# Where the output bias of an attention layer is added: in a TensorE bank, or in place by GpSimd

## The chip, the cores and the metric

The kernel runs on one core of one Trainium2 chip, in Bass: each engine's instructions are written out by hand in their order, and semaphores join them. The metric is the time of one launch in microseconds (us), as the median of several runs.

## The reference

A transformer block on x of 4096 rows (4 sequences of 1024) with 128 features, all in float32:

```
h  = layernorm(x)
q, k, v = h @ Wq + bq, h @ Wk + bk, h @ Wv + bv        # 16 heads of 8
q, k = q / |q|, k / |k|                                 # per head
attn = (q @ k.T) / 1024 ** sigmoid(m)                   # no softmax
x1 = x + (attn @ v) @ Wo + bo
h2 = layernorm(x1)
logits = h2 @ router.T                                  # 16 experts, one chosen per row
out = x1 + expert(h2 * sigmoid(top logit)) + shared(h2) # two gated MLPs
```

As there is no softmax, `(q @ k.T) @ v` is computed as `q @ (k.T @ v)`, with one masked 128x128 matrix per sequence that already holds Wo. The term of this case is `bo`, a row of 128 numbers that is added to every row of `x`.

## The kernel before, in words

The rows stand in 32 tiles of 128 rows, and four tiles make a quad; `c` is always a quad, 0 to 7. Two quads are one sequence. `xres` (128 partitions, 32 tiles, 128 features) holds x, later x1, and at last the output. Every step of a quad is a small function on one engine, and each engine calls these functions in an order written out by hand, the steps of several quads interleaved:

- VectorE: `x_stats(c)` (line 725) takes mean and variance of the quad's rows of `xres` with `bn_stats` and `bn_aggr` (lines 719 and 722) and raises `var1`. `take(c, h)` (line 757) scales half a quad's q, k and v out of PSUM and adds their biases. `head_sums` (765), `inv_norms` (770), `x1_stats` (735), `h_scales` (743) and, per quad, `choose` and `place`, which rank the rows for the experts, follow. `weights_lo(n)` (line 783) is done twice: it takes the low part of a weight matrix of the shared MLP, 128x512, from two tiles in SBUF. Of them, `weights_lo(0)` stands behind `x_stats(7)`, `h_scales(1)` and `mask_vk(1)`, and before `head_sums(4)`; `weights_lo(1)` behind `take(7, 1)`.
- GpSimd: some constants, then `scale_v` and `scale_q` (line 317), which multiply a quad's v and q by the inverse norms; `hT_lo` (327), `count` (334), `scatter` (343, one indirect DMA for a tile), and from 122 us `send` (352), 48 indirect DMAs.
- ScalarE: copies out of PSUM, square roots, `x1_copy(c)` (465), which brings x1 back from PSUM into `xres`, `norm_h(c)` (471), and the SiLU of the experts.
- TensorE: `project`, `v_by_k`, `fold_wo`, `turn_q`, `attend`, `turn_h`, `route`, then the matmuls of the MLPs. `free(after)` is a wait that makes sure that a PSUM bank may be written.

`attend(c)` builds x1 for a quad in one bank: a product of a column of ones with the row of biases (line 1148), a product of the identity with `xres` (1149), and q by the matrix (1154). For the first product VectorE prepares the bias once, in `bias_rows` (lines 892 to 900): as the product is made in float32r, the bias is split into a rounded row and the remainder, on two partitions. `bias_rows` stands behind `x_stats(0)` and `scale_mask()` follows it, then `x_stats(1)`.

The bias is loaded by ScalarE's DMA queue behind `m_col`, `w_qkv` and `w_o`. The queue of SP loads x and its transpose quad by quad. A wait on a semaphore holds all that its engine has behind it.

Of the kernel before, what the change touches and what calls it, by code (L numbers as in the profile page):

```python
# [7 lines left out]
ALU = mybir.AluOpType  # L8
ACT = mybir.ActivationFunctionType
AX = mybir.AxisListType  # L10
F32 = mybir.dt.float32
F32R = mybir.dt.float32r
I32 = mybir.dt.int32

P = 128


def build_block(nc, S, x, x_t, w_in, b_in, Wo, bo, m_col_in, router_t, gate_up, down, shared_gate, shared_up,
# [4 lines left out]
    _, NT, D = x.shape  # L23
# [6 lines left out]
    Q = 4  # L30
# [22 lines left out]
    with ExitStack() as ctx:  # L53
        def sb(name, shape, dt=F32):
            return ctx.enter_context(nc.sbuf_tensor(name, shape, dt))

        def sem(name):
            return ctx.enter_context(nc.semaphore(name))

        xres = sb("xres", [P, NT, D])  # L60
# [12 lines left out]
        ident = sb("ident", [P, P])  # L73
        before = sb("before", [P, P])
        ones = sb("ones", [P, P])
# [40 lines left out]
        with ExitStack() as attention:  # L116
            def sb_a(name, shape, dt=F32):
                return attention.enter_context(nc.sbuf_tensor(name, shape, dt))

            qkv = sb_a("qkv", [P, QRING, Q, QKV])  # L120
            sq = sb_a("sq", [P, Q, 2 * D])
            xT = sb_a("xT", [P, T])
            qT = sb_a("qT", [P, RING, Q * P])
            ss = sb_a("ss", [P, 2, Q, 2 * HEADS])
            rn = sb_a("rn", [P, 2, Q, 2 * HEADS])
            vkm = sb_a("vkm", [P, 2, D])
            wb = sb_a("wb", [P, 2, D])
            w_qkv = sb_a("w_qkv", [P, D + QKV])
            b_qkv = sb_a("b_qkv", [P, QKV])
            w_c = sb_a("w_c", [P, QKV])  # L130
            m_col = sb_a("m_col", [P, 1])
            m_tmp = sb_a("m_tmp", [P, 4])
            head_mask = sb_a("head_mask", [P, D])
            zeros = sb_a("zeros", [P, E, W])
            w_sh = sb_a("w_sh", [P, 2, SF])
            bo_in = sb_a("bo_in", [2, D])
            bo_top = sb_a("bo_top", [2, D], F32R)
            bo_two = sb_a("bo_two", [2, Q, D], F32R)
            two_col = sb_a("two_col", [2, 1])
            ones_r = sb_a("ones_r", [2, P], F32R)  # L140
        xg = sb("xg", [P, SLOTS, W])
        logit = sb("logit", [P, SLOTS])
        logit_silu = sb("logit_silu", [P, SLOTS])
# [11 lines left out]
        ps_hT, ps_qy, ps_vk, ps_log = bank  # L155
# [6 lines left out]
        ld_b, ld_bo, ld_wo, ld_wa = sem("ld_b"), sem("ld_bo"), sem("ld_wo"), sem("ld_wa")  # L162
        ld_rw, ld_sg, ld_su, ld_sd = sem("ld_rw"), sem("ld_sg"), sem("ld_su"), sem("ld_sd")

        k_col, k_id, k_pool, k_ids = sem("k_col"), sem("k_id"), sem("k_pool"), sem("k_ids")
# [2 lines left out]
        ach = sem("ach")  # L168
        m_step, mask_rdy = sem("m_step"), sem("mask_rdy")
        var1, std1, rstd1 = sem("var1"), sem("std1"), sem("rstd1")  # L170
        wc_mm, wc_rdy, bo_rdy = sem("wc_mm"), sem("wc_rdy"), sem("bo_rdy")
        hT_mm, hT_sb = sem("hT_mm"), sem("hT_sb")
        qkv_mm, qkv_sb, sq_done = sem("qkv_mm"), sem("qkv_sb"), sem("sq_done")
        ssum, floored, nrm, rn_rdy = sem("ssum"), sem("floored"), sem("nrm"), sem("rn_rdy")
# [93 lines left out]
        def _(pool):  # L268
            g = nc.gpsimd
# [5 lines left out]
            g.memset(before[:], 1.0)  # L275
            g.memset(ones[:], 1.0)
            g.memset(head_mask[:], 1.0)
            g.memset(two_col[:], 1.0)
            g.memset(run_mask[:], 1.0)
            g.memset(seen[:, 0], 0.0).then_inc(k_pool, 1)  # L280
            pool.wait_ge(k_pool, 1)
# [1 line left out]
                            pattern=[[-1, P]], channel_multiplier=1).then_inc(k_id, 1)  # L283

            g.affine_select(out=head_mask[:], in_=head_mask[:], compare_op=ALU.is_ge, fill=0.0, base=0,
                            pattern=[[-HD, HEADS], [0, HD]], channel_multiplier=1).then_inc(k_pool, 1)

            g.affine_select(out=before[:], in_=before[:], compare_op=ALU.is_gt, fill=0.0, base=0,
                            pattern=[[1, P]], channel_multiplier=-1)

            g.affine_select(out=two_col[:], in_=two_col[:], compare_op=ALU.is_gt, fill=0.0, base=0,
                            pattern=[[0, 1]], channel_multiplier=1)
            g.affine_select(out=run_mask[:], in_=run_mask[:], compare_op=ALU.not_equal, fill=0.0, base=0,
                            pattern=[[0, E], [1, Q]], channel_multiplier=0)
            pool.wait_ge(k_pool, 2)
# [2 lines left out]
                            pattern=[[HD, HEADS], [0, HD]], channel_multiplier=-1).then_inc(k_pool, 1)  # L298
# [20 lines left out]
            def scale_v(c):  # L319
                scale_heads(c, 2 * D, HEADS, v_rdy)  # L320

            def scale_q(c):
                scale_heads(c, 0, 0, q_rdy)

            def hT_lo(c):
                pool.wait_ge(hT_hi_rdy, c + 1)
                g.tensor_tensor(hT[:, 1, 512 * c:512 * c + 512], hT_full[:, 512 * c:512 * c + 512],  # L327
                                hT[:, 0, 512 * c:512 * c + 512].bitcast(F32), ALU.subtract).then_inc(hT_rdy, 1)
# [17 lines left out]
            def send(g):  # L346
                pool.wait_ge(yg_rdy, g + 1)
                for j in range(Q):
                    n = g * Q + j
                    if n >= 3:  # L350
# [2 lines left out]
                        out=y_back, out_offset=bass.IndirectOffsetOnAxis(ap=xg[:, n, D + 1:D + 2].bitcast(I32), axis=0),  # L353
                        in_=yg[:, g % YRING, j], in_offset=None, bounds_check=T - 1, oob_is_err=False).then_inc(y_sent[n % 3], 16)

            scale_v(0)
            scale_q(0)
            scale_v(1)
            scale_q(1)
            scale_v(2)  # L360
            scale_q(2)
            scale_v(3)
            scale_q(3)
            hT_lo(0)
            count(0)
            scale_v(4)
# [67 lines left out]
        def _(act):  # L434
# [1 line left out]
            act.dma_start(m_col[:], m_col_in).then_inc(ld_m, 16)  # L436
            act.dma_start(w_qkv[:], w_in).then_inc(ld_wa, 16)
            act.dma_start(w_o[:], Wo).then_inc(ld_wo, 16)
            act.dma_start(bo_in[:], bo.partition_broadcast(2)).then_inc(ld_bo, 16)
            act.dma_start(rwT[:], router_t).then_inc(ld_rw, 16)  # L440

            act.wait_ge(ld_m, 16)
# [265 lines left out]
        def _(dve):  # L708
            v = nc.vector
            links = [0]  # L710

            def link(ins):
                links[0] += 1
                ins.then_inc(dch, 1)
                dve.wait_ge(dch, links[0])
# [173 lines left out]
                dve.wait_ge(k_pool, 3)  # L889
                v.tensor_scalar(head_mask[:], head_mask[:], m_tmp[:, 3:4], None, ALU.mult).then_inc(mask_rdy, 1)  # L890

            def bias_rows():
                dve.wait_ge(ld_bo, 16)
                dve.wait_ge(k_ids, 1)
                v.tensor_copy(ones_r[:], ones[0:2, :])
                link(v.tensor_copy(bo_top[:], bo_in[:]))
                link(v.tensor_scalar(bo_top[:].bitcast(F32), bo_top[:].bitcast(F32), two_col[:], None, ALU.mult))
                v.tensor_tensor(bo_two[:], bo_in[:].unsqueeze(1).broadcast_to([2, Q, D]),
                                bo_top[:].bitcast(F32).unsqueeze(1).broadcast_to([2, Q, D]), ALU.subtract
                                ).then_inc(bo_rdy, 1)  # L900

            v.memset(zeros[:], 0.0).then_inc(z_done, 1)
            dve.wait_ge(ach, 1)
            link(v.tensor_scalar(m_tmp[:, 1:2], m_tmp[:, 0:1], 1.0, None, ALU.add))
            v.reciprocal(m_tmp[:, 2:3], m_tmp[:, 1:2]).then_inc(m_step, 1)
            x_stats(0)
            bias_rows()
            scale_mask()
            x_stats(1)
            x_scales(0)  # L910
# [183 lines left out]
        def _(pe):  # L1094
            te = nc.tensor
# [46 lines left out]
                last.then_inc(qT_mm, 1)  # L1142

            def attend(c, after=None):
                if c == 0:
                    pe.wait_ge(bo_rdy, 1)
                free(after)
                te.matmul(ps_qy[:], ones_r[:], bo_two[:].rearrange("p j d -> p (j d)"), start=True, stop=False)
                te.matmul(ps_qy[:], ident[:], xres[:, Q * c:Q * c + Q, :].rearrange("p j d -> p (j d)"), start=False,
                          stop=False)  # L1150
                pe.wait_ge(qT_sb, c + 1)
                pe.wait_ge(wb_rdy, c // QB + 1)
                for j in range(Q):
                    last = te.matmul(ps_qy[:, P * j:P * j + P], qT[:, c % RING, P * j:P * j + P], wb[:, c // QB % 2],
                                     start=False, stop=(j == Q - 1))
                last.then_inc(y_mm, 1)
# [334 lines left out]
```

## Time and profile before

| | |
|---|---|
| time, median of 3 runs | 216.1 us (215.64 to 216.8) |
| span of the profiled execution, first to last instruction | 212.6 us |
| the profiled execution's own time | not recorded beside its span; the median of the runs lies 3.5 us above the span |
| TensorE busy | 192.1 us (90%), 1126 matmuls |
| VectorE busy | 146.2 us (69%), 501 instructions |
| ScalarE busy | 103.2 us (49%), 234 instructions |
| GpSimd busy | 112.1 us (53%), 140 instructions |
| granted TensorE clock, mean | 0.998 of full speed |

The profile follows one execution. Busy time is the time in which an engine carried out an instruction; an engine's row of the timeline gives the start, the duration (of several instructions of one kind together, with their count), the line, the operation and the tiles, and in brackets how long the engine was idle before and what released it. PE is TensorE, DVE VectorE, ACT ScalarE, POOL GpSimd; a q behind an engine's name is its instruction queue.

### The profile page before, as it was taken

The numbers are of one execution on the slowest core, as the hardware profiler recorded it, in microseconds if no ns is written. First come the engines' busy times: TensorE is split into PE (matmuls) and PEld (weight loads), VectorE is DVE, ScalarE is ACT, GpSimd is POOL, SyncE is SP. The second block draws the span as 40 slices with busy tenths as digits, with TensorE's granted clock in tenths as the row PEclk, the third lists the DMA queues.
The fourth block names the chain that finished last, engine by engine and source line by source line (L and its number), as shares of the span: only waits on it lengthen the run. The fifth ranks groups of instructions, "written<-read, shape, count | busy, mean of one in ns | idle before, by whom it ended". The sixth has DMA issues, their size and how long they took to land.

```text
span 212.6 us, 3825 instructions
## 1 busy us (share of the span) xinstructions
PE 192.1 (90%) x1126; PEld 155.6 (73%) x1126; DVE 146.2 (69%) x501; ACT 103.2 (49%) x234; POOL 112.1 (53%) x140
## 2 busy tenths in 40 slices
PE   0896699999989899999988989999999999999992
PEld 0352556656767677888677979899999898889882
DVE  3679999999999977866535767946645333247553
ACT  3423464983567499773414556556653223122320
POOL 6002504357598787667720077777767777760000
PEclk9999999999999999999999999999999999999999
DMA  5999993000100101111125446621111110039243
GB/s 166 309 390 259 177 378 153 5 0 25 39 28 27 38 25 41 52 38 50 52 63 112 106 118 149 158 59 43 47 33 38 45 47 0 0 91 327 81 161 135
DMA packets 17607, 21.59 MB, mean 102 GB/s; under 512 B 3224, under 2 KB 11679, under 8 KB 17332
## 3 DMA queue, kind: packets, MB, share of 16 engines
q1 hardware_dynamic: 13872, 15.73, 26.4%
q0 software_dynamic: 2560, 4.24, 6.3%
q10 hardware_dynamic: 1156, 1.39, 1.9%
q8 instruction: 9, 0.15, 0.3%
q14 instruction: 10, 0.08, 0.1%
HBM read 13.95 MB, written 8.44 MB: 105 GB/s over the span
## 4 chain that ended last, share of the span: by engine, by line
PE 29%; DVE 28%; POOL 16%; issue 12%; DMA 8%; ACT 5%; POOLq 1%; ACTq 0%; DVEq 0%
POOL y_back L352 14%; PE bank L1222 8%; DVE qkv L757 7%; DMA y_back<-yg,xg 6%; DVE ss L765 4%; DVE st L719 4%; PE quad_banks L1200 3%; PE quad_banks L1202 3%; PE quad_banks L1201 3%; PE quad_banks L1115 3%; ACT h_rows L471 2%; DVE rn L770 2%; DMA w_qkv<-w_in 2%; PE quad_banks L1245 2%; DVE mv L722 2%
## 5 line engine op out<-in xcount | busy, mean ns | idle before, releaser
L352 POOL DMA_INDIRECT y_back<-yg,xg x48 | 47.3, 985 | 30.5 <-ACT yg L543 15.0
L842 DVE TENSOR_TENSOR s_act<-quad_banks,sg_act 128x512 f32<-128x512 f32 x32 | 22.0, 688 | 26.9 <-PE bank L1222 15.3
L515 ACT ACTIVATE sg_act<-quad_banks 128x512 f32<-128x512 f32 x32 | 19.2, 599 | 42.1 <-PE quad_banks L1202 42.1
L343 POOL DMA_INDIRECT x_slots<-h_rows,pos x32 | 31.6, 988 | 12.2 <-issue 6.2
L1222 PEld LDWEIGHTS bank<-sdT,s_act 128*128 128x128 f32 x256 | 31.8, 191 | 1.7
L1222 PE MATMUL bank<-sdT,s_act 128*128 128x128 f32 x256 | 32.9, 276 | 0.0
L317 POOL TENSOR_TENSOR qkv<-qkv,rn 128x512 f32<-128x512 f32 x16 | 17.0, 1079 | 28.0 <-DVE rn L770 27.9
L1115 PE MATMUL quad_banks<-w_c,xT 128*128 128x384 f32 x64 | 25.9, 544 | 2.0 <-DVE qkv L757 1.2
L1245 PE MATMUL quad_banks<-w_gu,xgT 128*128 x96 | 22.9, 382 | 0.8 <-ACT xgT L526 0.8
L1115 PEld LDWEIGHTS quad_banks<-w_c,xT 128*128 128x128 f32 x64 | 12.6, 212 | 11.3 <-issue 4.4
L1245 PEld LDWEIGHTS quad_banks<-w_gu,xgT 128*128 128x128 f32 x96 | 17.3, 190 | 2.9 <-issue 1.0
L757 DVE SCALAR_TENSOR_TENSOR qkv<-quad_banks,rs,b_qkv 128x384 f32<-128x384 f32 x32 | 17.7, 602 | 1.2 <-PE quad_banks L1115 1.0
L534 ACT ACTIVATE eg_act<-quad_banks,esc 128x128 f32<-128x128 f32 x48 | 13.7, 371 | 9.7 <-PE quad_banks L1245 8.9
L876 DVE SCALAR_TENSOR_TENSOR e_act<-quad_banks,esc,eg_act 128x128 f32<-128x128 f32 x48 | 13.5, 343 | 6.9 <-ACT eg_act L534 6.8
L1200 PE MATMUL quad_banks<-hT,sgT 128*128 128x512 f32 x32 | 14.8, 463 | 1.6 <-DVE s_act L842 1.3
L719 DVE BATCH_NORM_STATS2 st<-xres 128x6 f32<-128x128 f32 x64 | 13.7, 276 | 1.4 <-DMA xres<-L_attn_x 1.4
L471 ACT ACTIVATE h_rows<-xres,nm,rs 128x128 f32<-128x128 f32 x32 | 13.2, 485 | 2.0 <-DVE nm L743 2.0
L885 DVE COPY e_actT<-bank 128x512 f32<-128x512 f32 x12 | 8.3, 689 | 8.2 <-PE bank L1253 7.1
L327 POOL TENSOR_TENSOR hT<-hT_full,hT 128x512 fp32r<-128x512 f32 x8 | 10.7, 1356 | 3.8 <-ACT hT L481 3.7
L1264 PEld LDWEIGHTS bank<-w_dn,e_actT 128*128 128x128 f32 x96 | 12.3, 191 | 0.5
L1264 PE MATMUL bank<-w_dn,e_actT 128*128 x96 | 12.6, 275 | 0.0
L1202 PE MATMUL quad_banks<-hT,sgT 128*128 128x512 f32 x32 | 12.6, 395 | 0.0
(142 smaller groups left out, 364.5 us busy)
## 6 DMA issues: line engine op xcount, KB each, us to landing
xg<-x_slots SPq DMA_DIRECT2D x48, 65.0 KB, 2.0
xT<-x_t SPq DMA_DIRECT2D x8, 256.0 KB, 7.1
xres<-L_attn_x SPq DMA_DIRECT2D x8, 256.0 KB, 7.2
w_gu<-gate_up SPq DMA_DIRECT2D x1, 2048.0 KB, 14.7
h_rows<-y_back SPq DMA_DIRECT2D x8, 256.0 KB, 5.0
x_slots<-zeros SPq DMA_DIRECT2D x1, 1040.0 KB, 16.8
w_dn<-down SPq DMA_DIRECT2D x1, 1024.0 KB, 16.7
out<-xres SPq DMA_DIRECT2D x4, 256.0 KB, 2.2
```

What stands on the lines that cost most here:

```text
L343: g.indirect_dma_start(out=x_slots, out_offset=bass.IndirectOffsetOnAxis(ap=pos[:, t:t + 1], axis=0), in_=h_rows[:, t, :], in_offset=None) ...
L352: nc.gpsimd.indirect_dma_start(out=y_back, out_offset=bass.IndirectOffsetOnAxis(ap=xg[:, n, D + 1:D + 2].bitcast(I32), axis=0), in_=yg[:, ...
L515: a.activation(sg_act[:, n % 2], pair[:, 2 * (n % 2)], ACT.Silu).then_inc(s_silu, 1)
L719: last = v.bn_stats(st[:, t, :], xres[:, t, :])
L757: last = v.scalar_tensor_tensor(out=qkv[:, c % QRING, j, :], in0=pair[:, j, 0:QKV], scalar=rs1[:, t:t + 1], in1=b_qkv[:], op0=ALU.mult, op ...
L842: v.tensor_tensor(s_act[:, n % 2], pair[:, 2 * (n % 2) + 1], sg_act[:, n % 2], ALU.mult).then_inc(s_act_rdy, 1)
L1115: last = te.matmul(pair[:, j, 0:QKV], xT[:, P * (Q * c + j):P * (Q * c + j + 1)], w_c[:], start=True, stop=True)
L1200: te.matmul(to, lhs[:, 0], rhs[:, 0], start=True, stop=False)
L1202: return te.matmul(to, lhs[:, 1], rhs[:, 0], start=False, stop=True)
L1222: last = te.matmul(Y_BANK[c][:, here], s_act[:, n % 2, here], sdT[:, D * k:D * k + D], start=(k == 0 and j == 0), stop=(k == KC - 1 and j ...
L1245: mm = te.matmul(gate_up_banks(g % 2)[:, j, :], xgT[:, g % 2, P * j:P * j + P], gu_cols[:, bass.ds(held[g][j] * 2, F2)], start=True, stop= ...
L1264: mm = te.matmul(ps_yg[:, here], e_actT[:, g % 2, here], dn_cols[:, bass.ds(cols[j], D)], start=True, stop=True)
```

## The change

`bias_rows` and its product leave the kernel. The bias is loaded to all 128 partitions, and GpSimd adds it to `xres` in place, a quad at a time, once `x_stats` of that quad has read it. `attend` waits for that addition and starts its bank with the identity's product. The constant `two_col` goes as well, from GpSimd's preamble.

```
-            bo_in = sb_a("bo_in", [2, D])                 (and bo_top, bo_two, two_col, ones_r)
+            bo_in = sb_a("bo_in", [P, D])
...
-            g.memset(two_col[:], 1.0)
...
-            g.affine_select(out=two_col[:], in_=two_col[:], compare_op=ALU.is_gt, fill=0.0, base=0,
-                            pattern=[[0, 1]], channel_multiplier=1)
...
+            def add_bias(c):
+                if c == 0:
+                    pool.wait_ge(ld_bo, 16)
+                pool.wait_ge(var1, c + 1)
+                r = xres[:, Q * c:Q * c + Q, :]
+                g.tensor_tensor(r, r, bo_in[:].unsqueeze(1).broadcast_to([P, Q, D]), ALU.add).then_inc(x_bo, 1)
...
+            add_bias(0)
+            add_bias(1)
+            add_bias(2)
             scale_v(0)
             scale_q(0)
             scale_v(1)
             scale_q(1)
+            add_bias(3)
+            add_bias(4)
             scale_v(2)
             scale_q(2)
+            add_bias(5)
             scale_v(3)
             scale_q(3)
+            add_bias(6)
+            add_bias(7)
             hT_lo(0)
...
-            act.dma_start(bo_in[:], bo.partition_broadcast(2)).then_inc(ld_bo, 16)
+            act.dma_start(bo_in[:], bo.partition_broadcast(P)).then_inc(ld_bo, 16)
...
-            def bias_rows():                              (its nine lines, and its call behind x_stats(0))
...
             def attend(c, after=None):
-                if c == 0:
-                    pe.wait_ge(bo_rdy, 1)
-                free(after)
-                te.matmul(ps_qy[:], ones_r[:], bo_two[:].rearrange("p j d -> p (j d)"), start=True, stop=False)
-                te.matmul(ps_qy[:], ident[:], xres[:, Q * c:Q * c + Q, :].rearrange("p j d -> p (j d)"), start=False,
+                pe.wait_ge(x_bo, c + 1)
+                free(after)
+                te.matmul(ps_qy[:], ident[:], xres[:, Q * c:Q * c + Q, :].rearrange("p j d -> p (j d)"), start=True,
                           stop=False)
```

## Rows read from the trace of the kernel before

**Rows 1.** Busy us of PE, PEld, DVE, ACT, POOL in stretches; clock, DMA, GB/s.
```profile
42.00:52.00 10.00, 9.68 (x46) 5.97 (x46) 9.53 (x35) 6.71 (x16) 6.35 (x6) 1.00 0.02 7
...
62.00:73.60 11.60, 10.51 (x65) 8.18 (x65) 11.25 (x33) 6.00 (x14) 10.08 (x10) 1.00 0.09 29
...
88.00:100.00 12.00, 11.90 (x85) 10.95 (x86) 8.20 (x34) 7.14 (x14) 8.30 (x11) 1.00 0.15 50
...
122.00:186.00 64.00, 63.20 (x410) 57.21 (x409) 34.16 (x108) 29.89 (x81) 47.94 (x49) 1.00 0.24 62
```

**Rows 2.** Waits of VectorE from 8 to 76 us: us in total, times, longest.
```profile
DVE st L719 <- DMA xres<-L_attn_x: 1.2, 1, 1.2
DVE qkv L757 <- PE quad_banks L1115: 1.0, 1, 1.0
DVE ss L765 <- ACT sq L487: 0.2, 1, 0.2
```

**Rows 3.** The chain that ended last, 73 to 89 us: start, us, what.
```profile
73.60 1.66 ACT h_rows L471 x4
...
80.87 0.53 ACT xres L465
...
83.50 0.43 PE bank L1148
...
86.39 1.66 ACT h_rows L471 x4
...
88.10 0.66 PE bank L1162 x4
```

**Rows 4.** Timeline of ScalarE: x1_copy(7).
```profile
85.91 0.59 ACT L465 COPY xres<-bank 128x512 f32<-128x512 f32 x1 [0.91 <-PE bank L1154]
```

**Rows 5.** Timeline of VectorE: the scales of quad 6 for norm_h(6).
```profile
85.56 0.58 DVE L743 TENSOR_SCALAR nm<-mv,rs 128x1 f32<-128x1 f32 x4
```

**Rows 6.** Timeline of VectorE from 6.9 to 14 us.
```profile
6.95 0.21 DVE L895 CAST ones_r<-ones 2x128 fp32r<-2x128 f32 x1 [0.25 <-DMA bo_in<-L_attn_bo]
...
7.65 0.68 DVE L898 TENSOR_TENSOR bo_two<-bo_in,bo_top 2x512 fp32r<-2x512 f32 x1
...
9.72 0.87 DVE L719 BATCH_NORM_STATS2 st<-xres 128x6 f32<-128x128 f32 x4 [1.19 <-DMA xres<-L_attn_x]
...
13.42 1.14 DVE L757 SCALAR_TENSOR_TENSOR qkv<-quad_banks,rs,b_qkv 128x384 f32<-128x384 f32 x2 [1.04 <-PE quad_banks L1115]
```

**Rows 7.** The DMA issue of bo (timeline of ScalarE), and issues by tile (KB, us to landing).
```profile
2.22 0.54 ACTq L439 DMA_DIRECT2D bo_in<-L_attn_bo  x1
...
b_qkv<-b_in SPq DMA_DIRECT2D x1, 192.0 KB, 5.7
```

**Rows 8.** Timeline of GpSimd from 19 to 45 us.
```profile
19.96 2.11 POOL L317 TENSOR_TENSOR qkv<-qkv,rn 128x512 f32<-128x512 f32 x2 [15.54 <-DVE rn L770]
...
32.37 2.11 POOL L317 TENSOR_TENSOR qkv<-qkv,rn 128x512 f32<-128x512 f32 x2 [6.85 <-DVE rn L770]
36.70 2.12 POOL L317 TENSOR_TENSOR qkv<-qkv,rn 128x512 f32<-128x512 f32 x2 [2.23 <-DVE rn L770]
42.55 1.79 POOL L327 TENSOR_TENSOR hT<-hT_full,hT 128x512 fp32r<-128x512 f32 x1 [3.73 <-ACT hT L481]
```

**Rows 9.** Timeline of VectorE: half a take beside scale_v(1).
```profile
23.34 1.14 DVE L757 SCALAR_TENSOR_TENSOR qkv<-quad_banks,rs,b_qkv 128x384 f32<-128x384 f32 x2
```

**Rows 10.** Timeline of VectorE: the end of x_stats(7), and weights_lo(0).
```profile
41.35 0.38 DVE L722 BATCH_NORM_AGGREGATE mv<-st 128x2 f32<-128x6 f32 x4
...
42.52 0.68 DVE L783 TENSOR_TENSOR sgT<-w_sh,sgT 128x512 fp32r<-128x512 f32 x1
```

**Rows 11.** Timeline of GpSimd: scatter(8) and hT_lo(2).
```profile
66.17 1.01 POOL L343 DMA_INDIRECT x_slots<-h_rows,pos  x1 [0.15 <-issue]
67.19 1.28 POOL L327 TENSOR_TENSOR hT<-hT_full,hT 128x512 fp32r<-128x512 f32 x1
```

**Rows 12.** Timeline of VectorE: weights_lo(1).
```profile
66.78 2.25 DVE L783 TENSOR_TENSOR suT<-w_sh,suT 128x512 fp32r<-128x512 f32 x1
```

More of the change, by code:

```diff
@@ L135, in build_block @@
             w_sh = sb_a("w_sh", [P, 2, SF])
[L136 to L140, printed above, removed]
+            bo_in = sb_a("bo_in", [P, D])
         xg = sb("xg", [P, SLOTS, W])
@@ L170, in build_block @@
         var1, std1, rstd1 = sem("var1"), sem("std1"), sem("rstd1")
-        wc_mm, wc_rdy, bo_rdy = sem("wc_mm"), sem("wc_rdy"), sem("bo_rdy")
+        wc_mm, wc_rdy, x_bo = sem("wc_mm"), sem("wc_rdy"), sem("x_bo")
         hT_mm, hT_sb = sem("hT_mm"), sem("hT_sb")
@@ L890, in scale_mask @@
                 v.tensor_scalar(head_mask[:], head_mask[:], m_tmp[:, 3:4], None, ALU.mult).then_inc(mask_rdy, 1)
[L892 to L900, printed above, removed]
             v.memset(zeros[:], 0.0).then_inc(z_done, 1)
@@ L906, in _ @@
             x_stats(0)
-            bias_rows()
             scale_mask()
```

## The prediction

> **What bounds the kernel now.** Three views, in this order. First the busy times by stretch: from 42 to 73.6 us VectorE is busy 9.53 of 10.00 and 11.25 of 11.60 us, from 88 to 186 us TensorE 11.90 of 12.00 and 63.20 of 64.00 [rows 1]. So there are two halves with different bounds, and the bias work of the diff lies wholly in the first. Second, VectorE's waits from 8 to 76 us: there are three, of 1.2, 1.0 and 0.2 us [rows 2], and the last, before the second head_sums, ends at 20 us. Nothing that TensorE, ScalarE or GpSimd do between 20 and 73 us holds it up; what is added to its own stream there is not made good again. Third, the chain that ended last: at 73.60 us it leaves VectorE for norm_h(4) on ScalarE, passes attend(7) on TensorE at 83.50 us, norm_h(6) at 86.39 us and turn_h(6) at 88.10 us [rows 3]. From there TensorE and, from 122 us, GpSimd's sends and TensorE side by side carry it to the end; both start from where this chain stands, so a shift at 73.6 us comes out whole at the end, and one in attend(7) as far as turn_h(6) feels it.
>
> **TensorE: eight bias products go.** One costs 0.43 us of TensorE's time, the step from its start to the next matmul's in the chain [rows 3]; eight are 3.4 us. Those of attend(0) to attend(5) lie before 73.6 us, where VectorE waits for nobody: they become TensorE idle time, worth nothing. That of attend(6) is followed by x1_copy(6), which the chain reaches at 80.87 us from ScalarE's own work before it, not from TensorE [rows 3]: nothing. That of attend(7) is on the chain. x1_copy(7) had waited 0.91 us for it and began at 85.91 us [rows 4]; 0.43 us earlier it begins at 85.48 and, with the 0.48 us to its successor (86.39 less 85.91), norm_h(6) could begin at 85.96. But norm_h(6) also needs the scales of its quad, which VectorE ends at 85.56 + 0.58 = 86.14 us [rows 5]. So it begins near 86.18 instead of 86.39: a gain of 0.2 us, 0.43 at most if VectorE moves up too. Each attend now waits for x_bo before its first matmul; behind that wait stand all of TensorE's later matmuls, so it must never come last. It does not: the latest, for quad 7, is given near 43 us (below) and asked for at 83.5. As a satisfied wait it costs between 0 and the 0.2 us of the gain; no row shows one by itself, and I take 0.
>
> **VectorE: bias_rows goes.** Its four instructions run from 6.95 to 7.65 + 0.68 = 8.33 us, 1.4 us in all. Behind them VectorE sat idle for 1.19 us until x's second quad landed at 9.72 us, and after that again 1.04 us for TensorE's second projection, to 13.42 us [rows 6]. Both idle times stand in front of the stretch without waits; removing the four only lengthens the first. Worth 0. If that cover were gone it would be worth 1.4 us at most, but the second idle time belongs to TensorE's projections, which the diff does not touch.
>
> **The load of bo.** 64 KB instead of 1 KB, 128 rows of 512 bytes, behind w_qkv and w_o on ScalarE's queue. The nearest row is b_qkv, the same kind of broadcast at three times the size: 5.7 us from issue to landing [rows 7]. Issued at 2.22 us, bo is there by some 8 us, an estimate from that row, and the first attend asks for it after 20. How much it delays the loads of x's quads no row shows by itself. A third of b_qkv's 5.7 us, 1.9, is an upper end, as if nothing else had moved meanwhile; VectorE has 1.04 us in hand before 13.42 us [rows 6], so the cost lies between 0 and 0.9 us. I take 0, because b_qkv shared its 5.7 us with the loads around it.
>
> **GpSimd: eight additions come.** Of 128x512 elements each; the nearest instruction is scale_heads with the same shape and also one broadcast operand, 2.11 us for two, so 1.06 us [rows 8]; the other one, hT_lo with two full operands, runs 1.28 undisturbed [rows 11]. That makes 8.5 us, or 10.2 at the upper bound. add_bias(0) to (2) follow x_stats(0) to (2); scale_v(0) starts at 19.96 after 15.54 us of idle time, and between x_stats(2) and its release VectorE has two halves of take to do, 1.14 us each [rows 6], and two more steps: more than add_bias(2)'s 1.06. (3) and (4) lie in the 6.85 us before 32.37. (5) runs from 34.48 to 35.54 and scale_v(3) starts at 36.70: 1.16 us to spare. (6) runs at 38.82. (7) waits for x_stats(7) and runs from about 41.81 to 42.87; hT_lo(0), which ran from 42.55 to 44.34, moves to 42.87 and, at 1.28 us, ends no later than it did [rows 8, 11]. No product of GpSimd comes late. A VectorE instruction that reads PSUM or one tile of SBUF does not feel GpSimd: take costs 1.14 us for two at 23.34 us beside scale_heads [rows 9] and 1.14 at 13.42 beside nothing [rows 6].
>
> **The collision.** One VectorE instruction in GpSimd's new stretch is of another kind: weights_lo, with both inputs in SBUF. Twice it met a GpSimd tensor operation. At 42.52 us it came 0.03 us ahead of hT_lo(0) and took its 0.68 us, while hT_lo(0) took 1.79 [rows 8, 10] instead of 1.28. At 66.78 us it came while GpSimd was in scatter(8), hT_lo(2) followed at 67.19 without a gap, and weights_lo took 2.25 us, to 69.03: 0.56 us past the end of hT_lo(2) at 68.47 [rows 11, 12]. It got nothing until both were through. The Trainium skill, SBUF — State Buffer, Who interferes with whom, has the rule: a VectorE instruction with two SBUF inputs and a GpSimd instruction that reads SBUF take a shared read port in turn, whole instructions at a time, whichever was first. Both meetings agree with the first half of it. Taken at its word, whoever asks first would go first, and a waiting weights_lo would be let in ahead of GpSimd's next instruction, which is rival (a); the second meeting, 2.25 us, speaks against that half.
>
> After the change, x_stats(7) releases add_bias(7) at 41.35 + 0.38 = 41.73, and weights_lo(0) comes at 42.52 [rows 10], 0.35 us before add_bias(7) is through. hT_lo(0) is then ready (its input was there at 42.55) and follows at once, to 42.87 + 1.28 = 44.15. If it goes as at 66.78 us, weights_lo(0) ends at 44.15 + 0.56 = 44.71 instead of 42.52 + 0.68 = 43.20: 1.5 us. If VectorE is let in between, it ends at 42.87 + 0.6 = 43.47: 0.3 us. Both fall in the stretch where VectorE has no slack. I take 1.5, since the nearest meeting went so.
>
> **Sum.** 212.6 us of span, less 0.2, plus 1.5: 213.9. The trace gives no total for this execution beyond its span; the median of the runs, 216.1, lies 3.5 above it. So 217.4 us. The likeliest case by itself runs from 217.0 (0.43 gained, the stall 1.3) to 217.8 (additions of 1.28 us, no gain from attend(7)).
>
> **Rivals.**
> (a) VectorE slips in between add_bias(7) and hT_lo(0): 216.1 + 0.3 - 0.2 = 216.2. For it: it would only be the order of arrival. Against: 66.78 us.
> (b) No stall, as the two do not meet: 216.1 - 0.2 = 215.9, or 215.7 with the full 0.43. For it: no row shows weights_lo beside an addition of float32 tiles. Against: add_bias(7) and weights_lo(0) hang on the same VectorE stream, 0.8 us apart, so they do meet, and hT_lo reads SBUF as the addition does.
> (c) Clearly faster: the stall that exists already, at 66.78 us, is undone by the new order. It cost 2.25 - 0.68 = 1.6 us. It goes if weights_lo(1) comes before scatter(8) (0.6 us earlier against GpSimd) and no stall comes at 42.5: 216.1 - 1.6 - 0.2 = 214.3. Against: scale_v(6), scatter(8) and weights_lo(1) all follow one VectorE instruction. The whole 3.4 us of TensorE, 212.7, would need TensorE to be the bound before 73 us, and rows 1 and 2 say no.
> (d) Worse: add_bias(5) takes longer than its 1.06 + 1.16 us of room, scale_v(3) and what follows come about 1 us late beside the stall: 218.5. No row has such a GpSimd operation beyond 1.79.
>
> **Chances.** Forecast 0.53, (a) 0.17, (b) 0.10, (c) 0.14, (d) 0.06. The range of 215.0 to 218.4 leaves out (c) and half of (d), 0.17 in all, and holds the forecast with the 0.9 us of the load. A measurement tells 0.5%, about 1.1 us, from no change: the bounds are 215.0 and 217.2. The forecast lies just past the upper one, so I count 0.33 of its 0.53 as slower and 0.20 as same. Slower 0.33 + 0.06 = 0.39, same 0.20 + 0.17 + 0.08 = 0.45, faster 0.14 + 0.02 from (b) = 0.16.
>
> **What would show it.** After the change the first weights_lo should take about 2.2 us near 42.5 and stand behind two GpSimd tensor operations without a gap; norm_h(4) should start near 75.1 instead of 73.6; the wait for x_stats(1)'s load should grow from 1.2 to about 2.5 us; the gap of ScalarE before x1_copy(7) should shrink by about 0.4. A first weights_lo of 0.7 us, or a first attend that waits on GpSimd, would make the prediction wrong in its mechanism; a VectorE that waits on something between 44 and 73 us would make it wrong in how the stall reaches the end.

## The result, and the profile after

| | before | after |
|---|---|---|
| time, median | 215.57 us (10 runs, 214.6 to 218.55) | 218.58 us (10 runs, 216.9 to 222.24) |
| ratio, 95% interval | | 1.0144 [1.0112, 1.0176] |
| VectorE, instructions | 501 | 497 |
| GpSimd busy | 112.1 us | 121.8 us |
| TensorE matmuls | 1126 | 1118 |

Slower, by 1.4%. The forecast was 217.4 us with a range of 215.0 to 218.4: the direction was right, the size and most of the cause were not. The spans of the two traces, 212.6 and 219.3 us, differ by 6.7 us where the medians differ by 3.0; so the traces are compared stretch by stretch, not by their spans. Below, "after" is the changed kernel.

The forecast's own place comes first. Timeline of GpSimd and of VectorE near 42 us in the changed kernel (start, us, engine, line, operation, tiles; in brackets the idle time before it):

```profile
41.59 1.28 POOL L323 TENSOR_TENSOR xres<-xres,bo_in 128x512 f32<-128x512 f32 x1 [1.77 <-DVE mv L730]
42.81 1.73 POOL L327 TENSOR_TENSOR hT<-hT_full,hT 128x512 fp32r<-128x512 f32 x1
```
```profile
42.30 1.12 DVE L791 TENSOR_TENSOR sgT<-w_sh,sgT 128x512 fp32r<-128x512 f32 x1
43.34 1.21 DVE L773 TENSOR_REDUCE ss<-sq 128x128 f32<-128x1024 f32 x1
```

`weights_lo(0)` (L791) and `add_bias(7)` (L323) met as expected, but VectorE was let in between the addition and `hT_lo(0)` (L327): 1.12 us instead of 0.68, and `hT_lo(0)` is the one that waited, 1.73 us. Here the cost is 0.44 us, not 1.5 [rows 10].

Yet `norm_h(4)` starts at 75.81 us, 2.21 later than before [rows 3], and the forecast gave it 1.5. The missing part lies further on. VectorE's waits from 8 to 78 us in the changed kernel (us in total, times, longest):

```profile
DVE st L727 <- DMA xres<-L_attn_x: 3.4, 1, 3.4
DVE qkv L765 <- PE quad_banks L1112: 0.5, 1, 0.5
DVE qkv L765 <- issue: 0.4, 1, 0.4
DVE ss L773 <- ACT sq L495: 0.2, 1, 0.2
```

The third line is new against [rows 2]: VectorE stands still for 0.38 us at 55.5 us, and the trace names nobody for whom it waits. Then a second stall that the kernel before did not have. VectorE and GpSimd in the changed kernel:

```profile
55.88 1.14 DVE L765 SCALAR_TENSOR_TENSOR qkv<-quad_banks,rs,b_qkv 128x384 f32<-128x384 f32 x2 [0.38 <-issue]
...
62.07 1.95 DVE L807 TENSOR_TENSOR_SCAN incl<-run_mask,hot 128x64 f32<-128x64 f32 x1
...
68.98 2.26 DVE L791 TENSOR_TENSOR suT<-w_sh,suT 128x512 fp32r<-128x512 f32 x1
```
```profile
55.77 0.96 POOL L343 DMA_INDIRECT x_slots<-h_rows,pos  x1 [0.90 <-DVE pos L818]
...
61.61 0.96 POOL L343 DMA_INDIRECT x_slots<-h_rows,pos  x1 [0.30 <-issue]
62.59 1.27 POOL L327 TENSOR_TENSOR hT<-hT_full,hT 128x512 fp32r<-128x512 f32 x1
```

The same rows of the kernel before:

```profile
61.50 0.29 DVE L799 TENSOR_TENSOR_SCAN incl<-run_mask,hot 128x64 f32<-128x64 f32 x1
```
```profile
56.42 0.96 POOL L343 DMA_INDIRECT x_slots<-h_rows,pos  x1 [1.74 <-DMA x_slots<-h_rows,pos]
...
62.26 0.96 POOL L343 DMA_INDIRECT x_slots<-h_rows,pos  x1 [0.30 <-issue]
63.25 1.27 POOL L327 TENSOR_TENSOR hT<-hT_full,hT 128x512 fp32r<-128x512 f32 x1
```

The running sum of `choose(2)` (the scan, with both inputs in SBUF) took 0.29 us and was over 0.47 us before scatter(7) began. After the change it comes during scatter(7), with `hT_lo(1)` next in GpSimd's order, and takes 1.95 us, until 0.16 us past the end of `hT_lo(1)`: 1.66 us more. Two shifts brought them together: VectorE 0.57 us later (61.50 to 62.07), GpSimd 0.65 us earlier (62.26 to 61.61), and the latter begins at scatter(4), which waits 0.90 us instead of 1.74. 0.44 + 0.38 + 1.66 = 2.48 us; between the starts of `weights_lo(0)` and `norm_h(4)` 2.43 us more went by (33.51 against 31.08).

The third loss is at the end. GpSimd and TensorE in the changed kernel, and its stretches there (us, then busy us of PE, PEld, DVE, ACT, POOL, then the granted clock, DMA share, GB/s):

```profile
191.85 2.54 POOL L327 TENSOR_TENSOR hT<-hT_full,hT 128x512 fp32r<-128x512 f32 x2
```
```profile
193.20 0.50 PE L1195 MATMUL quad_banks<-hT,sgT 128*128 128x512 f32 x1 [2.07 <-POOL hT L327]
```
```profile
186.00:194.00 8.00, 5.93 (x34) 5.00 (x33) 2.67 (x4) 1.79 (x3) 6.78 (x7) 1.00 0.02 0
194.00:198.00 4.00, 4.00 (x16) 3.51 (x15) 0.69 (x1) 0.60 (x1) 0.39 (x1) 0.57 0.91 279
198.00:206.00 8.00, 8.00 (x52) 7.09 (x51) 4.38 (x7) 2.17 (x4) 0.00 (x0) 1.00 0.52 191
```

`hT_lo(6)` stands behind the sends in GpSimd's order, the first of which went out at 125.65 us (122.57 before), and TensorE waited 2.07 us for it. The kernel before has these lines too:

```profile
186.67 2.54 POOL L327 TENSOR_TENSOR hT<-hT_full,hT 128x512 fp32r<-128x512 f32 x2
```
```profile
188.02 0.50 PE L1200 MATMUL quad_banks<-hT,sgT 128*128 128x512 f32 x1 [0.22 <-POOL hT L327]
```

From the first send to `hT_lo(6)` GpSimd took 66.20 us in the changed kernel and 64.10 before; TensorE came to its wait 65.48 us after the first send, and 65.23 before. So the wait is not the earlier shift, which moves both engines alike: the sends themselves took 2.10 us longer. In part they wait longer for earlier sends to land, 9.8 us in all against 8.9; why, no run shows.

After its 2.07 us of idle time TensorE was granted 0.57 of its clock for 4 us, that is mostly 1.2 GHz, and did 16 matmuls in them, where 52 took the next 8 us at 2.4 GHz. What other runs have of this only their mean granted clocks tell: the two runs of after with 0.997 and 1.0 took 216.90 and 216.96 us, the other eight, with 0.991 and less, 218.15 us and more, the one in the trace 221.13. Of the 6.7 us between the spans, 2.21 lie ahead of `norm_h(4)`, 0.87 between there and the first send, and 3.62 behind that; the medians differ by only 3.0, so the usual run has less than this trace.

### The profile page after: what moved, and what is told of

Its sections match the earlier page's. It is cut to its first block, busy times and chain, and to the rows that moved or that the text cites. A ratio compares the mean times of both kernels' runs of the same rounds, so it can differ in the third digit from the quotient of the medians.

```text
span 219.3 us, 3818 instructions
## 1 busy us (share of the span) xinstructions
PE 191.0 (87%) x1118; PEld 155.5 (71%) x1118; DVE 146.6 (67%) x497; ACT 103.1 (47%) x234; POOL 121.8 (56%) x146
## 4 chain that ended last, share of the span: by engine, by line
PE 29%; DVE 29%; DMA 11%; issue 10%; POOL 10%; SPq 5%; ACT 3%; POOLq 1%; ACTq 0%; DVEq 0%
DVE qkv L765 7%; POOL y_back L352 7%; PE quad_banks L1240 6%; PE bank L1217 5%; SPq L245 4%; DMA y_back<-yg,xg 4%; DVE ss L773 4%; DMA x_slots<-h_rows,pos 4%; DVE st L727 4%; PE quad_banks L1195 3%; PE quad_banks L1196 3%; PE quad_banks L1197 3%; PE quad_banks L1112 2%; PE bank L1259 2%; DVE rn L778 2%
## 5 line engine op out<-in xcount | busy, mean ns | idle before, releaser
L1217 PEld LDWEIGHTS bank<-sdT,s_act 128*128 128x128 f32 x256 | 32.7, 196 | 1.9 <-DVE s_act L850 0.2
L1217 PE MATMUL bank<-sdT,s_act 128*128 128x128 f32 x256 | 33.7, 280 | 0.0
L1195 PE MATMUL quad_banks<-hT,sgT 128*128 128x512 f32 x32 | 15.1, 472 | 4.2 <-POOL hT L327 2.5
L542 ACT ACTIVATE eg_act<-quad_banks,esc 128x128 f32<-128x128 f32 x48 | 13.7, 371 | 9.5 <-PE quad_banks L1240 8.7
L323 POOL TENSOR_TENSOR xres<-xres,bo_in 128x512 f32<-128x512 f32 x8 | 10.1, 1270 | 10.8 <-DVE mv L730 5.9
L727 DVE BATCH_NORM_STATS2 st<-xres 128x6 f32<-128x128 f32 x64 | 13.7, 276 | 3.5 <-DMA xres<-L_attn_x 3.5
L1197 PE MATMUL quad_banks<-hT,suT 128*128 128x512 f32 x32 | 12.9, 402 | 0.0
L1196 PE MATMUL quad_banks<-hT,sgT 128*128 128x512 f32 x32 | 12.8, 401 | 0.0
L1197 PE MATMUL quad_banks<-hT,sgT 128*128 128x512 f32 x32 | 12.7, 398 | 0.0
```

The costliest lines, as they stand in the source:

```text
L727: last = v.bn_stats(st[:, t, :], xres[:, t, :])
L1195: te.matmul(to, lhs[:, 0], rhs[:, 0], start=True, stop=False)
L1196: te.matmul(to, lhs[:, 0], rhs[:, 1], start=False, stop=False)
L1197: return te.matmul(to, lhs[:, 1], rhs[:, 0], start=False, stop=True)
L1217: last = te.matmul(Y_BANK[c][:, here], s_act[:, n % 2, here], sdT[:, D * k:D * k + D], start=(k == 0 and j == 0), stop=(k == KC - 1 and j ...
```

## The experiments

Times are medians; the ratio, with its 95% interval, is to the kernel before, run on the same chip at the same time. Where two experiments are compared, their medians can be from different chips; the kernel before took 215.53 to 215.89 us beside them.

**e1, the change without its additions.** All that is removed stays removed, and the larger load of bo stays; the output lacks the bias.

```
-            add_bias(0)                     (and the seven others)
...
-                pe.wait_ge(x_bo, c + 1)
```


> The changed kernel without GpSimd's eight additions and without the wait for them; the bias is left out of the output. What stays of the change is TensorE's eight products gone, VectorE's bias_rows gone and the large load of bo. Theory 1 (a shared port: additions delay weights_lo(0), and the shift then puts the scan of choose(2), 1.95 us instead of 0.29, behind scatter(7) and hT_lo(1)): weights_lo(0) takes 0.68 us, the scan 0.29, norm_h(4) starts within 0.3 us of the kernel before (73.6), time 0 to 0.5 us below the kernel before. Rival (the shift comes from what was removed or from the load, not from the additions): the scan still takes about 1.9 us, norm_h(4) starts near 75.5, time 1 to 3 us above the kernel before.

217.91 us, 1.0103 [1.0046, 1.016]. VectorE of this kernel:

```profile
42.74 0.68 DVE L783 TENSOR_TENSOR sgT<-w_sh,sgT 128x512 fp32r<-128x512 f32 x1
...
55.91 1.14 DVE L757 SCALAR_TENSOR_TENSOR qkv<-quad_banks,rs,b_qkv 128x384 f32<-128x384 f32 x2 [0.38 <-issue]
```

The stall at 42 us is gone, the idle time and the scan's (62.10 us, 1.96) are not, and most of the loss remains. The theory that the additions do it fell here. What is left is what was taken away, or the larger load; e5 decides between them.

**e2, the additions without the removal.** The kernel before with the larger load, and with eight additions that write a spare tile.

```
+                g.tensor_tensor(x_spare[:], r, bo_in[:].unsqueeze(1).broadcast_to([P, Q, D]), ALU.add).then_inc(x_bo, 1)
...
+                pe.wait_ge(x_bo, c + 1)
```


> The kernel before with the large load of bo and the eight additions on GpSimd, at the places of the change, but into a spare tile that nobody reads; attend waits for them, the bias product and bias_rows stay. Theory 1: weights_lo(0) takes about 1.1 us, the scan of choose(2) comes late enough to stand behind hT_lo(1), time 1.5 to 3 us above the kernel before. Rival (removals or load are what matters): the time is within 0.5 us of the kernel before.

218.01 us, 1.0116 [1.0069, 1.0164], and not a clean test: `bias_rows` now waits for the larger load and VectorE is over a microsecond late from the start (`weights_lo(0)` at 43.69 us); with the 0.54 us of the table below, `norm_h(4)` starts 1.71 us later than before. What it does show: 1.17 us for `weights_lo(0)`, no idle time near 55 us, 0.29 us for the scan.

**e3, `hT_lo(1)` moved behind `count(2)`**, which waits for the scan, so that the two cannot meet.

```
-            hT_lo(1)
             count(2)
+            hT_lo(1)
```


> The changed kernel with hT_lo(1) behind count(2) on GpSimd; count(2) waits for the scan of choose(2), so hT_lo(1) can no longer stand in front of it. Theory 1: the scan takes 0.29 us, norm_h(4) starts 1.5 to 1.7 us earlier than in the changed kernel (75.8), the time falls by about 1.6 us against it. Rival (the loss lies after 120 us: GpSimd's sends end late, TensorE waits for hT_lo(6) near 191 us and then runs some 3 us at 1.2 GHz): the scan is short, but the time falls by less than 0.5 us, because the wait and the slow clock stay.

216.81 us, 1.0043 [1.0003, 1.0083]; the scan takes 0.29 us. 1.8 us less than after.

**e4, `hT_lo(5)` to `(7)` moved ahead of `send(0)`**, so that TensorE's last products don't wait for the sends (`hT_lo(5)` stood before `send(10)`, the other two behind `send(11)`).

```
             hT_lo(4)
+            hT_lo(5)
+            hT_lo(6)
+            hT_lo(7)
             send(0)
```


> The changed kernel with hT_lo(5) to hT_lo(7) moved in front of GpSimd's sends, into its 15 us of idle time from 107 to 123 us. Sends theory (TensorE's wait for hT_lo(6) near 191 us, 2.07 us in the profile of the changed kernel, and the slow clock behind it): the wait is gone, the clock of 194 to 200 us is 1.00 instead of 0.72, the time falls by 1.5 to 3.5 us against the changed kernel and its spread shrinks. Theory 1 alone (all that matters is lost before 76 us): the time falls by less than 0.5 us.

217.04 us, 1.0063 [1.0025, 1.0101]: 1.5 us less than after. The scan still takes 1.98 us and `norm_h(4)` starts at 76.39, but TensorE no longer waits and keeps its clock of 1.00 from 190 to 200 us.

**e8, both moves.**

```
             count(2)
+            hT_lo(1)                        (from ahead of it)
...
+            hT_lo(5)                        (and 6 and 7, from behind their sends)
             send(0)
```


> The changed kernel with the moves of the two earlier trials together: hT_lo(1) behind count(2), and hT_lo(5) to hT_lo(7) in front of the sends; hT_lo(2) stays. Theory (scan and wait for hT_lo(6) are separate losses): 1.6 us less than with only the latter move (217.04), so about 215.4 to 216, within 0.5% of the kernel before. Rival (the two are one loss seen twice): the same as with either move alone, 216.8 to 217.

215.19 us, 0.9982 [0.9944, 1.002], 3.4 us less than after: the gains of the two moves, 1.8 and 1.5 us, are separate and add up.

**e11, the same two moves in the kernel before.**

> The kernel before with the two moves that brought the changed kernel from 218.58 to 215.19 us: hT_lo(1) behind count(2), and hT_lo(5) to (7) ahead of send(0). Theory (the two losses belong to the change): the scan of choose(2) takes 0.29 us as it did, the wait for hT_lo(6) was only 0.22 us, so little is gained: 215.0 to 215.8, norm_h(4) near 73.6, and the changed kernel with the same moves is within 0.5 us of it. Rival (the moves help any order of this program, and undo a loss that the kernel before had too): 213 or less; then the changed kernel is still 2 us behind under equal moves, and a part of its loss is unexplained.

214.39 us, 0.9942 [0.9905, 0.9979]. Neither theory's number: the moves also gain 1.1 us here, where the scan was never held and TensorE waited only 0.22 us; so of the 3.4 us that they gain in the changed kernel 2.3 belong to the change. Under equal moves the change costs 0.4% (0.9982 against 0.9942), or 0.8 us, which these intervals do not tell from nothing. It is the size of the two pieces that the moves leave in place, 0.44 + 0.38 us.

**e5, VectorE's stream kept as long as before.** Four instructions of the kind of `bias_rows`, which nobody uses, in its old place.

```
+                v.tensor_copy(ones_r[:], ones[0:2, :])
...
             x_stats(0)
+            dead_rows()
```


> The changed kernel with four dead instructions on VectorE where bias_rows stood (same kinds, same waits in number, no wait for bo), so that VectorE's stream is as long as before. Instruction theory: with bias_rows gone, the place where VectorE's stream is loaded on moves from behind head_sums(5), where it was hidden, to the front of take(6, 0), where it costs 0.38 us, and the 8 KB load at 54.3 us that made scatter(2) land late moves too, so that scatter(4), scatter(7) and hT_lo(1) come 0.65 us earlier and meet the scan of choose(2). With the count restored: no 0.38 us of idle time before take(6, 0), scatter(4) again waits about 1.7 us for scatter(2), the scan takes 0.29 us, norm_h(4) starts near 73.8 and the time is 1.5 to 2.5 us below the changed kernel. Rival (TensorE's missing products bring the shift): idle time, the short wait of scatter(4) and the scan of 1.95 us all stay, norm_h(4) near 75.8, time as the changed kernel.

216.59 us, 1.0042 [1.0003, 1.0082], 2.0 us less than after with more work. The additions, the larger load and the missing products of TensorE are all still there. VectorE in this kernel has no idle time at 55 us, and the scan is itself again:

```profile
55.16 1.14 DVE L768 SCALAR_TENSOR_TENSOR qkv<-quad_banks,rs,b_qkv 128x384 f32<-128x384 f32 x2
...
61.36 0.29 DVE L810 TENSOR_TENSOR_SCAN incl<-run_mask,hot 128x64 f32<-128x64 f32 x1
```

So it is `bias_rows` missing from VectorE that costs. The four bring back both the length of the stream and their own time, and no run tells these apart; but the take near 13.4 us starts at the same time in the kernel before and in the changed one (13.42 and 13.40), so the time alone is not what reaches 55 us.

**e9, `add_bias(7)` behind `hT_lo(0)`.**

```
-            add_bias(7)
             hT_lo(0)
+            add_bias(7)
```


> The changed kernel with add_bias(7) behind hT_lo(0) instead of ahead of it. Theory (the meeting of weights_lo(0) with add_bias(7) is a small part, 0.2 to 0.5 us; the scan at 62 us and the late last sends make the rest): weights_lo(0) arrives near 42.3 us with no addition running, takes 0.7 us or, if it comes during hT_lo(0), 1.1; the scan of choose(2) still takes about 1.95 us and norm_h(4) still starts at 75.4 to 75.9; time 218.1 to 218.6, no more than 0.4 below the changed kernel's 218.58. Rival (the forecast's place): the order around add_bias(7) is what costs: 217.1 or less, norm_h(4) below 74.5.

217.26 us, 1.0068 [1.0025, 1.011]. The stretch went much as the theory said (0.68 us for `weights_lo(0)`, 1.95 for the scan; `norm_h(4)` at 76.17, where it had 75.4 to 75.9), the time did not: 0.8 us below what it expected. In the trace the end is shorter than in after: TensorE waits 1.15 us for `hT_lo(6)` and keeps its clock from 180 to 204 us. No run shows why.

**e10, `hT_lo(2)` ahead of scatter(8)**, so that `weights_lo(1)` comes during a tensor operation of GpSimd instead of a scatter.

```
-            scatter(8)
             hT_lo(2)
+            scatter(8)
```


> The changed kernel with hT_lo(2) ahead of scatter(8) instead of behind it. weights_lo(1) then arrives near 69 us while GpSimd is in hT_lo(2), a tensor operation, with scatter(8) and scatter(9) behind it; before, it arrived during scatter(8) with hT_lo(2) behind and took 2.26 us. Theory (arriving during a GpSimd tensor operation, VectorE is served next; arriving during a scatter, it is passed by the next tensor operation): weights_lo(1) takes about 1.1 to 1.3 us, norm_h(4) starts about 1 us earlier (74.8), time about 217.4. Rival 1 (it waits for whatever GpSimd has queued without a gap): 2.2 us or more, no gain. Rival 2 (it is a matter of distance in time alone, not of what GpSimd is in): anything between 0.7 and 2.2, without the value of 1.1 to 1.3 seen at weights_lo(0).

217.21 us, 1.0118 [1.0019, 1.0216]. GpSimd and VectorE of this kernel:

```profile
68.31 1.27 POOL L327 TENSOR_TENSOR hT<-hT_full,hT 128x512 fp32r<-128x512 f32 x1
69.74 1.27 POOL L343 DMA_INDIRECT x_slots<-h_rows,pos  x1 [0.16 <-issue]
```
```profile
69.13 1.00 DVE L791 TENSOR_TENSOR suT<-w_sh,suT 128x512 fp32r<-128x512 f32 x1
```

1.00 us instead of 2.26, a little under the 1.1 to 1.3 expected: it ends 0.55 us after `hT_lo(2)`, just as the first `weights_lo` ends 0.54 to 0.55 us after `add_bias(7)` in the eight kernels where those two meet. It confirms the theory in this stretch; the time, with its wide interval, does not tell this kernel from after.

**e6 and e7, all the meetings apart**, in the changed kernel and in the one before: the two moves of e8, and `hT_lo(2)` behind scatter(9).

```
-            hT_lo(2)
             scatter(9)
+            hT_lo(2)
```


> The changed kernel with three moves on GpSimd: hT_lo(1) behind count(2), hT_lo(2) behind scatter(9), hT_lo(5) to hT_lo(7) in front of the sends. Theory (the losses are meetings on the shared port and the wait for hT_lo(6)): the scan of choose(2) takes 0.29 and weights_lo(1) 0.7 us instead of 2.25, norm_h(4) starts near 72.9, the time is 0.5 to 2 us below the kernel before. If a scatter by itself blocks weights_lo(1), this takes about 1.2 us and the gain is 0.5 us smaller. Rival (TensorE's lower load, and with it the clock, is the main loss): the two instructions are short, but the time stays 1 us or more above the kernel before.

> The kernel before with the same three moves on GpSimd. Theory: weights_lo(1) takes 0.7 us instead of 2.25, norm_h(4) starts near 72.0 instead of 73.6, and 1.5 to 2.5 us are gained against the kernel before. Rival (TensorE, busy 99% from 122 to 186 us, takes the gain back): norm_h(4) is earlier, but the time falls by less than 0.5 us.

214.06 us, 0.9892 [0.9818, 0.9966], and 213.82 us, 0.9872 [0.9784, 0.996]; four runs each. Both beat both kernels, and whether the bias is added by GpSimd or by TensorE no longer shows in the time of four runs; in the first half of the traces e6 is still 0.78 us longer (table below). GpSimd and VectorE of the kernel before with these moves:

```profile
66.67 1.01 POOL L343 DMA_INDIRECT x_slots<-h_rows,pos  x1 [0.15 <-issue]
67.99 0.96 POOL L343 DMA_INDIRECT x_slots<-h_rows,pos  x1 [0.30 <-issue]
```
```profile
67.29 0.68 DVE L783 TENSOR_TENSOR suT<-w_sh,suT 128x512 fp32r<-128x512 f32 x1
```

`weights_lo(1)` comes in the middle of scatter(8) and takes its plain 0.68 us, where it had taken 2.25 [rows 12]. So the scatter itself does not hold it; the tensor operation behind the scatter does.

**All thirteen traces in one table.** Column 2 runs from the start of `weights_lo(0)` to that of `norm_h(4)`. Column 3 is how much more than in the kernel before that is. Column 4 adds up the excess of `weights_lo(0)` over 0.68, the idle time at 55 us, the scan's excess over 0.29 and that of `weights_lo(1)` over 2.25. Then the wait of TensorE for `hT_lo(6)` and the time from the first send to the end of the span.

| | us | more | four pieces | wait | to the end |
|---|---|---|---|---|---|
| before | 31.08 | | | 0.22 | 90.0 |
| after | 33.51 | +2.43 | 0.44+0.38+1.66+0.01 | 2.07 | 93.7 |
| e1 | 33.12 | +2.04 | 0+0.38+1.67+0.01 | 2.10 | 93.3 |
| e2 | 31.62 | +0.54 | 0.49+0+0+0 | 0.76 | 90.3 |
| e3 | 31.88 | +0.80 | 0.43+0.38+0+0 | 1.03 | 90.3 |
| e4 | 33.56 | +2.48 | 0.43+0.38+1.69+0.01 | none | 89.4 |
| e5 | 31.51 | +0.43 | 0.43+0+0+0.01 | 2.07 | 93.2 |
| e6 | 30.28 | -0.80 | 0.43+0.38+0-1.57 | none | 89.0 |
| e7 | 29.50 | -1.58 | 0+0+0-1.57 | none | 90.0 |
| e8 | 31.85 | +0.77 | 0.43+0.38+0+0.01 | none | 89.0 |
| e9 | 33.08 | +2.00 | 0+0.38+1.66+0.01 | 1.15 | 90.5 |
| e10 | 32.24 | +1.16 | 0.43+0.38+1.66-1.25 | 1.38 | 91.0 |
| e11 | 31.15 | +0.07 | 0 | none | 89.5 |

In the first half the four pieces account for every kernel to 0.07 us. At the end there are two groups: the three kernels in which TensorE waited 2.07 to 2.10 us took 93.2 to 93.7 us, and in all three the granted clock fell to 0.57 to 0.59 over four microseconds behind that wait; the ten with 1.38 us or less took 89.0 to 91.0, with the clock at 1.00 there. So in these three traces a wait of 2 us came with over 2 us more than any other kernel has. The wait does not follow the shift of the first half: it is 2.07 us in e5 with +0.43, and 1.15 in e9 with +2.00. It goes rather with the landing of the sends: GpSimd waited 9.8 to 11.2 us in all for earlier sends in these three, and 7.7 to 8.9 in the other five that keep `hT_lo(6)` in its place. Between `norm_h(4)` and the first send lie 48.9 to 51.2 us, in no order that the edits explain. Most of that spread lies ahead of the copy of the row table (`take_table`, line 835 of the kernel before): from its start to the first send it is 16.3 to 16.9 us in all thirteen.

## Why the prediction was wrong

The median rose by 3.0 us; the sum had 1.5 - 0.2 = 1.3. By the experiments' medians the 3.0 are 0.8 that stay under equal moves (e8 against e11), 1.8 for the scan (e3), and 0.4 at the end (the 1.5 of e4 less the 1.1 of e11), the last no larger than the differences between medians of one kernel. By its steps:

- **What bounds the kernel**: right. The four pieces are all VectorE's, in the stretch without waits, and each came out whole at `norm_h(4)`. Too strong was that nothing GpSimd does there holds VectorE up: the 2.25 us of `weights_lo(1)` [rows 12] are such a hold, which shows as a long instruction and not in the list of waits [rows 2].
- **Eight products of TensorE**: right as far as `turn_h(6)`. From `norm_h(4)` to `turn_h(6)` 14.11 us instead of 14.50 went by, a gain of 0.39, at the upper end of the 0.2 to 0.43 given. `x1_copy(7)` had to wait 0.38 us instead of 0.91, and `norm_h(6)` then came as the scales ended, at 88.21, as the step said. ScalarE and VectorE of the changed kernel, to set beside [rows 4, 5]:

```profile
87.52 0.59 ACT L473 COPY xres<-bank 128x512 f32<-128x512 f32 x1 [0.38 <-PE bank L1149]
88.21 1.65 ACT L479 ACTIVATE h_rows<-xres,nm,rs 128x128 f32<-128x128 f32 x4
```
```profile
87.60 0.58 DVE L751 TENSOR_SCALAR nm<-mv,rs 128x1 f32<-128x1 f32 x4
```

  That the gain reaches the end no run shows: the chain that ended last no longer passes `norm_h(6)` in the changed kernel, but GpSimd's scatters and their landings (start, us, what):

```profile
84.74 0.98 POOL x_slots L343
...
87.29 3.34 DMA x_slots<-h_rows,pos
```

- **The load of bo**: right in its cost, 0. It landed 6.9 us after its issue, near 9.1 us and not by 8. `x_stats(1)` waits 3.35 us and starts at 10.20 instead of 9.72, and the take that follows starts at 13.40 against 13.42 [rows 6]: the second idle time took it up. VectorE of the changed kernel:

```profile
10.20 0.87 DVE L727 BATCH_NORM_STATS2 st<-xres 128x6 f32<-128x128 f32 x4 [3.35 <-DMA xres<-L_attn_x]
...
13.40 1.14 DVE L765 SCALAR_TENSOR_TENSOR qkv<-quad_banks,rs,b_qkv 128x384 f32<-128x384 f32 x2 [0.54 <-PE quad_banks L1112]
```

- **GpSimd's additions**: 1.27 us each, 10.1 in all, the upper bound and not the 1.06 taken; hidden as said, with 1.01 us left ahead of `scale_v(3)`. The group of these instructions (busy us, mean ns, idle time before them), and two rows of GpSimd's timeline:

```profile
L323 POOL TENSOR_TENSOR xres<-xres,bo_in 128x512 f32<-128x512 f32 x8 | 10.1, 1270 | 10.8 <-DVE mv L730 5.9
```
```profile
34.21 1.26 POOL L323 TENSOR_TENSOR xres<-xres,bo_in 128x512 f32<-128x512 f32 x1
36.48 2.11 POOL L310 TENSOR_TENSOR qkv<-qkv,rn 128x512 f32<-128x512 f32 x2 [1.01 <-DVE rn L778]
```

- **The collision**: the two met, but at 0.44 us. That was rival (a). I let the one long meeting of the trace [rows 12] decide, where GpSimd was in a scatter when VectorE came, for a place where it is in a tensor operation. Arriving during a tensor operation VectorE was next in all nine cases (the first `weights_lo` in after, e2 to e6, e8 and e10, the second in e10: 1.00 to 1.17 us). Arriving during a scatter with a ready tensor operation behind it, it was passed: the scan in after, e1, e4, e9 and e10, `weights_lo(1)` in all but e6, e7 and e10 (1.95 to 2.26 us). The Trainium skill, SBUF — State Buffer, Who interferes with whom, has it that the order of issue decides who blocks; the meetings of the first kind agree (1.00 us in e10), those of the second don't, if a row's start tells the order of issue, for there VectorE's row starts 0.4 to 0.5 us before that of `hT_lo` and still waits for its end.
- **"VectorE: bias_rows goes ... Worth 0"**: this is the step that failed. Its 1.4 us were indeed worth nothing, but I costed only their time. Shortening VectorE's stream brought the idle 0.38 us and moved GpSimd 0.65 us forward, and so the scan onto `hT_lo(1)`: 2.04 of the 2.43 us, and e1, without the additions, shows just those 2.04. The four dead instructions of e5 undo both.
- **"a shift at 73.6 us comes out whole at the end"**: as far as medians tell, it did for the scan (e3: 1.66 us in the trace, 1.8 us of time); for the 1.57 us of `weights_lo(1)` the medians of four runs show 1.1 (e6 against e8) and 0.6 (e7 against e11), too few runs to decide. But the step put nothing at the end itself. Behind 122 us the sends and TensorE run side by side; I did not ask which of them would be late for the other at 188 us, where the trace already showed a wait of 0.22. In the trace of after it is 2.07 us, with a stretch at 1.2 GHz behind it, and e4 takes it away, for 1.5 us. That the change makes this wait is not shown: it does not follow the shift, and the moves gain 1.1 us in the kernel before as well (e11).

My test named in advance, "a VectorE that waits on something between 44 and 73 us would make it wrong in how the stall reaches the end", is what came.

**What stays open.** How a shorter stream of VectorE makes the two shifts. What the traces show is a transfer of 8 KB of instructions, on queue q14, at 54.30 us in the kernel before and at 56.46 in the changed one. Queue q14 from 54 to 54.5 us in the kernel before, and from 56 to 56.5 in the changed one (packets, MB, share of 16 engines):

```profile
q14 instruction: 1, 0.01, 3.8%
```
```profile
q14 instruction: 1, 0.01, 7.1%
```

In the kernel before it falls together with scatter(2)'s packets, for whose landing scatter(4) then waits 1.74 us. With `bias_rows` or its dead copies in place (before, e2, e5, e7, e11) it comes 11.4 to 12.3 us after the start of `weights_lo(0)`, scatter(4) waits 1.33 to 1.80 us, and there is no idle time; without them (the other eight) it comes 13.7 to 14.4 us after, scatter(4) waits 0.87 to 0.90, and VectorE is idle for 0.38. A second transfer of that queue comes at 52.0 to 58.7 us in the kernels with additions and at 65.5 to 69.2 in the others; which is which is read from these times. That the stream loaded in the first is VectorE's is inferred from this. The idle time is not a wait for that transfer itself, which starts 0.6 to 0.9 us after the idle time is over. Open as well: why the last sends take longer in some kernels, why the two moves gain 1.1 us in the kernel before (e11), and the lowered clock elsewhere in single runs.

## What to carry to other kernels

An instruction that is off the critical path still has a place in its engine's stream: taking it out can shift the others by half a microsecond, so look, for some microseconds to each side, for pairs that now miss each other narrowly, above all a VectorE operation with two SBUF inputs and a GpSimd tensor operation that stands right behind an indirect DMA. Such a pair is better parted in the order of the program than left to timing; e6 and e7 do that and, with the move at the end, gain about 1%. And where a short instruction that another engine waits for stands behind a long row of DMA issues that it does not need, as `hT_lo(6)` behind the sends, moving it ahead is worth trying: it took 1.5 us off the changed kernel (e4).

## What the runs showed of the hardware

A scan over 64 columns with both inputs in SBUF is held up by GpSimd like a 512-wide addition: 0.29 us alone, 1.95 behind `hT_lo(1)`. What GpSimd is in when VectorE comes matters more than whose row starts first: 0.02 us ahead of `hT_lo(0)` while GpSimd was idle, `weights_lo(0)` took 0.68 us (e9); 0.41 us ahead of `hT_lo(2)` while GpSimd was in a scatter, `weights_lo(1)` took 2.26. And the 128x512 addition with a broadcast row costs GpSimd 1.27 us, where its product with a broadcast of norms costs 1.08.
